# Decoder layers on one core: a first-layer FFN of three products of rounded halves, smaller rings, an expert's weights loaded early

## The reference

```python
# layer 0 (norm first), N_HEAD = 16, DK = 16
h = layernorm(x);  x = x + attn(h, h, causal=True)
h = layernorm(x);  x = x + attn(h, context, causal=False)
h = layernorm(x);  x = x + (relu(h @ ffn_w1 + ffn_b1) @ ffn_w2 + ffn_b2)     # 256 -> 1024 -> 256
# layer 1 (norm last)
x = layernorm(x + attn(x, x, causal=True))
x = layernorm(x + attn(x, context, causal=False))
x = layernorm(x + moe(x))       # router, 2 of 8 experts a row, each gelu(x @ w1 + b1) @ w2 + b2
```

## Time and profile before

| | us |
|---|---|
| median of 3 runs | 1222.42 |
| lowest, highest | 1221.40, 1225.18 |
| the profiled execution | 1223.96 |
| its span (first to last instruction) | 1222.2 |
| TensorE busy in it | 1092.2 (89%) |
| VectorE, ScalarE, GpSimd busy | 823.1, 729.8, 513.1 |

### The profile page before, as it was taken

How to read it: one execution, slowest core, us unless ns; L and a number is a source line. 1 busy time by engine, 2 the same in 40 slices (tenths; PEclk the granted TensorE clock), 3 DMA queues, 4 the chain that set the end, 5 groups by cost and what they waited for, 6 DMA issues and landing times. The chain is left out here.

```text
span 1222.2 us, 26984 instructions
## 1 busy us (share of the span) xinstructions
PE 1092.2 (89%) x8941; PEld 900.1 (74%) x8941; DVE 823.1 (67%) x2495; ACT 729.8 (60%) x1537; POOL 513.1 (42%) x732
## 2 busy tenths in 40 slices
PE   7688889999999999998999988887879999999960
PEld 7366667768887787876777766655669999999960
DVE  2677878775655555546777777764358888888856
ACT  4355565665555455445566666544339888988942
POOL 4355555331222213334667256442242444544544
PEclk9699999999999999999999999987889999999985
DMA  7774848554344434434756645540566878887764
GB/s 176 154 118 75 118 82 108 93 84 59 43 62 65 66 53 54 71 51 56 152 86 93 92 71 92 88 84 28 201 227 204 241 231 231 248 236 232 234 185 146
DMA packets 110313, 152.35 MB, mean 125 GB/s; under 512 B 23040, under 2 KB 94976, under 8 KB 103424
## 3 DMA queue, kind: packets, MB, share of 16 engines
q1 hardware_dynamic: 99984, 138.64, 51.9%
q0 software_dynamic: 8352, 10.80, 4.5%
q10 hardware_dynamic: 1872, 1.60, 1.0%
HBM read 78.39 MB, written 21.62 MB: 82 GB/s over the span
## 5 line engine op out<-in xcount | busy, mean ns | idle before, releaser
L929 ACT ACTIVATE probs<-s 128x384 f32<-128x384 f32 (+1 forms) x512 | 263.7, 542 | 187.5 <-PE s L727 173.4
L1001 DVE TENSOR_REDUCE neg_max<-s 128x2 f32<-128x512 f32 x256 | 169.2, 689 | 94.8 <-PE s L702 89.8
L727 PE MATMUL s<-q_stack,k_stack 98*128 98x256 bf16 (+1 forms) x1024 | 177.1, 263 | 17.4 <-ACT probs L929 16.3
L585 POOL TENSOR_SCALAR_AFFINE_SELECT probs<-probs 128x256 f32<-128x256 f32 x256 | 101.1, 407 | 174.0 <-ACT probs L929 174.0
L998 DVE CUSTOM_DVE_ANT_0 s<-s,mask_qk 128x256 f32<-128x256 f32 x256 | 114.0, 445 | 83.8 <-PE s L699 77.8
L727 PEld LDWEIGHTS s<-q_stack,k_stack 98*128 98x128 bf16 x1024 | 90.8, 99 | 42.9 <-ACT probs L929 27.3
L746 PE MATMUL pv<-probs,v 128*32 128x256 f32 (+1 forms) x2048 | 115.2, 367 | 2.0 <-POOL probs L585 1.8
L1363 PE MATMUL moe<-rows_hi,e_w_hi 128*128 128x256 f32 x368 | 104.1, 283 | 4.1 <-DVE rows_lo L1474 4.1
L702 PE MATMUL s<-k_stack,q_stack 96*128 96x256 bf16 x512 | 98.2, 276 | 10.0 <-DVE neg_max L1001 8.3
L1363 PE MATMUL moe<-e_w_hi,e_hidden_hi 128*128 128x256 f32 x368 | 104.8, 285 | 0.0
L1363 PE MATMUL moe<-rows_hi,e_w_lo 128*128 128x256 f32 x368 | 103.6, 281 | 0.0
(11 more groups left out here) (195 smaller groups left out, 2638.5 us busy)
## 6 DMA issues: line engine op xcount, KB each, us to landing
w<-in_expert_w SPq DMA_DIRECT2D x26, 1024.0 KB, 5.1
k_stack<-k_part SPq DMA_DIRECT2D x192, 128.0 KB, 4.1
e_w<-in_expert_w SPq DMA_DIRECT2D x24, 1024.0 KB, 5.4
q_stack<-q_part SPq DMA_DIRECT2D x180, 128.0 KB, 5.9
rows<-slots_x SPq DMA_DIRECT2D x25, 256.0 KB, 2.7
slots_x<-filler SPq DMA_DIRECT2D x8, 518.0 KB, 4.2
cT<-in_context SPq DMA_DIRECT2D x16, 256.0 KB, 5.3
e_b<-in_expert_b SPq DMA_DIRECT2D x24, 128.0 KB
```

The source lines that it names most:

```text
L585: pool.affine_select(out=blocks, in_=blocks, compare_op=ALU.is_ge, fill=0.0, base=0, pattern=[[0, TILES], [1, P]], channel_multiplier=-1). ...
L727: last = pe.matmul(dst[:, kt * S:kt * S + S - q0], k[:, kt * P:(kt + 1) * P], q[:, q0:S], start=True, stop=True)
L929: act.activation(probs[hd][:, 0:width], s2[hd % 2][:, 0:width], ACT.Exp, scale=SCALE).then_inc(probs_ready, 1)
L1001: dve.tensor_reduce(neg_max[:, :, hd], src[:].rearrange("p (t s) -> p t s", t=TILES), AX_X, ALU.max, negate=True).then_inc(s1_free, 1)
```

## The change

- The FFN's products become three float32r products of halves each, as in the expert part. The weights are halved once, in 8 pieces (`halve`: ScalarE rounds, VectorE subtracts), due beside the last calls of c = 0. The transposed rows (`hT_hi`, `hT_lo`) and the hidden values (`hidden_hi`, `hidden_lo`) are halved for each lane: a rounding on ScalarE and a subtraction on VectorE behind T, and behind each `up`.
- `both_kinds` gives one stretch of memory two names, one float32 and one float32r. The rests are written in place: `w1_lo`, `w2_lo`, `hT_lo` and `hidden_lo` lie over `w1`, `w2`, `hT_ffn` and `hidden`; `w1_hi`, `w2_hi` lie over `w1_next`, `w2_next`. The ReLU of the next lane therefore waits for the last `down` of the lane before.
- To make room: 12 `probs` for 16, 2 contexts for 3, one `h` and one `u` for two, `v` packed to 17 columns a head for 32, the FFN's normed rows in the attention's `o`, and the output biases of c = 2 and 3 loaded over those of c = 0 and 1.
- The weights of expert 1 go into `w1_next`, `w2_next` (the place of the FFN's rounded weights), loaded in four pieces of 512 KB beside calls (3, 2) and (3, 4).
- Due times, lags and paces change, and lane 0 of c = 3 is moved ahead of the last two lanes of c = 2.

```diff
@@ -56,30 +56,32 @@
-CONTEXTS = 3
+CONTEXTS = 2
+PROBS = 12
+VW = DK + 1
...
-LAG = {"scalar": {"T": 0.0, "q": 1.4, "k": 1.7, "v": 1.9, "out_T": 0.1, "up": 1.4, "head": 0.6, "shift": 0.5, "final_T": 0.5, "out": 1.4, "scale": 2.4},
-       "vector": {"max": 0.5, "q": 2.2, "k": 1.9, "shift": 2.8, "wo": 1.6, "down": 0.4, "turn": 0.7, "ln": 0, "apply": 3.6, "router": 0.6, "rank": 1.0, "pick": 0.6,
-                  "place": 0.6},
-       "gpsimd": {"mask": 0.6, "bias": 1.5, "ln": 0, "gain": 3.4, "q": 3.7, "k": 2.9, "scatter": 0},
-       "sync": {"q": 5.2, "k": 5.8, "shift": 0.5, "store": 0.2, "fetch": 0, "context": 0}}
-AT = {"later": 0.0, "pick": 65.9, "place": 68.60000000000001, "shares": (68.5, 71.5, 74.0, 79.3), "fill": 79.0, "ln": -7.3, "T": -1.9, "q": 0.4, "k": -0.8,
-      "v": 6.4, "bias": 10.4, "context": 8.3, "max": 14.8, "shift": 28.3, "head": 32.8, "weigh0": 43.7, "weigh1": 50.0, "turn": 52.5, "out_T": 55.0,
-      "wo": 56.5, "ffn_ln": 59.5, "ffn_T": 62.8, "ffn_bias": 67.4, "up": (68.0, 73.3, 75.1, 76.7), "down": (79.0, 81.5), "final_ln": 59.3, "final_T": 64.7,
-      "store": 63.1, "router": 65.5, "rank": 67.8, "scatter": 85.5, "post_ln": -16.4}
+LAG = {"scalar": {"T": 0.0, "q": 1.4, "k": 1.8, "v": 1.9, "out_T": 0.1, "up": 1.0, "head": 0.6, "shift": 0.8, "final_T": 0.5, "out": 1.4, "scale": 2.4, "halve": 0},
+       "vector": {"max": 0.5, "q": 1.8, "k": 1.9, "shift": 2.8, "wo": 0.4, "down": 0.8, "turn": 0.7, "ln": 0, "apply": 3.1, "router": 0.6, "rank": 1.0, "pick": 0.8,
+                  "place": 0.5, "up": 3.0, "T": 2.0, "halve": 1.0},
+       "gpsimd": {"mask": 0.6, "bias": 0, "ln": 0.5, "gain": 3.1, "q": 3.7, "k": 2.9, "scatter": 0},
+       "sync": {"q": 5.2, "k": 5.8, "shift": 0.5, "store": 0, "fetch": 0.3, "context": 0}}
+AT = {"later": 0.0, "pick": 65.8, "place": 68.6, "shares": (68.5, 71.3, 74.4, 77.0), "fill": 79.0, "ln": -7.5, "T": -1.9, "q": 0.5, "k": -0.8, "v": 6.4,
+      "bias": 13.1, "context": 8.9, "max": 14.8, "shift": 28.1, "head": 32.8, "weigh0": 43.7, "weigh1": 50.0, "turn": 52.5, "out_T": 55.1, "wo": 56.5,
+      "ffn_ln": 59.5, "ffn_T": 62.8, "ffn_bias": 67.4, "up": (65.5, 68.2, 72, 75), "down": (78.5, 81.0), "final_ln": 59.3, "final_T": 64.6, "store": 63.1,
+      "router": 65.5, "rank": 67.8, "scatter": 85.5, "post_ln": -15.0}
...
-PACE = {"max": 0.77, "head": 1.06}
-FETCH = {"w": 5, "ffn": 6.4, "contexts": 2, "qk": 18.0, "vo": 60.0, "expert": 8.2}
-CALL_OF_SLOT = "00000000111111112222222233333333"
+PACE = {"max": 0.71, "head": 1.06}
+FETCH = {"halves": 1.4, "apart": 3.0, "w": 4.5, "ffn": 5.6, "contexts": 0.5, "qk": 21.0, "vo": 60.7, "expert": 8.2}
+CALL_OF_SLOT = "00000000111111112222223223333333"
...
-FFN_LATER = [0.0, 0.0, 0.0, 0.0, 0.0, 0.0, 0.0, 0.0]
+FFN_LATER = [0, 0, 0.0, 0.0, 0, 0, 0, 0.0]
@@ -137,8 +139,10 @@
+    steps += [(at(1, 0) - SLOT * FETCH["halves"] + FETCH["apart"] * i, "halve", 0, i) for i in range(FC)]
...
+    steps += [(at(3, 2 + 2 * i) + 8.0, "fetch", 0, ("second expert", i)) for i in range(KC)]
@@ -238,13 +250,16 @@
-        v = ring(3, "v", [P, TILES, H, 2 * DK])
-        h = ring(2, "h", [P, TILES, D])
+        v = ring(3, "v", [P, TILES * H * VW + 2 * DK - VW])
+        h = sb("h", [P, TILES, D])
...
-        h_of = {FFN: sb("h_ffn", [P, TILES, D])}
-        hT_of = dict.fromkeys((FFN, FINAL), sb("hT_ffn_final", [P, KC, S]))
-        u = ring(2, "u", [P, H // 4, S])
+        (hT_ffn, hT_lo), (hidden, hidden_lo) = both_kinds(ctx, nc, "hT_ffn_final", [P, KC, S]), both_kinds(ctx, nc, "hidden", [P, FC, S])
+        hT_of = dict.fromkeys((FFN, FINAL), hT_ffn)
+        hT_hi, hidden_hi = sb("hT_hi", [P, KC, S], F32R), sb("hidden_hi", [P, FC, S], F32R)
+        (w1, w1_lo), (w2, w2_lo) = w1, w2
+        (w1_next, w1_hi), (w2_next, w2_hi) = w1_next, w2_next
+        u = sb("u", [P, H // 4, S])
@@ -279,11 +294,11 @@
-        probs = ring(H, "probs", [P, TILES * S])
+        probs = ring(PROBS, "probs", [P, TILES * S])
...
+        h_of = {FFN: o}
...
-        hidden = sb("hidden", [P, FC, S])
@@ -385,9 +405,18 @@
+        def piece_of_weights(i):
+            f = slice(2 * (i % 4), 2 * (i % 4) + 2)
+            cols = slice(2 * P * (i % 4), 2 * P * (i % 4 + 1))
+            return (w1[:, :, cols], w1_hi[:, :, cols], w1_lo[:, :, cols]) if i < 4 else (w2[:, f, :], w2_hi[:, f, :], w2_lo[:, f, :])
...
+        def probs_of(n, hd):
+            return probs[(n * H + hd) % PROBS]
@@ -436,6 +465,10 @@
+                elif what[0] == "second expert":
+                    i, half = what[1], FC // 2
+                    sp.dma_start(w1_next[:, i, :], t["expert_w1"][:, KC + i, :]).then_inc(expert_loaded, 16)
+                    sp.dma_start(w2_next[:, i * half:(i + 1) * half, :], t["expert_w2"][:, FC + i * half:FC + (i + 1) * half, :]).then_inc(expert_loaded, 16)
@@ -800,23 +838,29 @@
+            def pair_products(dst, lhs, rhs, first, end):
+                for m, (a, b) in enumerate(((0, 0), (1, 0), (0, 1))):
+                    last = pe.matmul(dst, lhs[a], rhs[b], start=first and m == 0, stop=end and m == 2)
+                return last
             def up(lane, j):
...
-                        pe.wait_ge(loaded_ffn, 16 * 2)
-                    pe.wait_ge(hT_ready, nth("T", lane, FFN))
+                        pe.wait_ge(w_low, FC)
+                    pe.wait_ge(hT_lo_ready, lane + 1)
...
-                        last = pe.matmul(dst[:, m * S:(m + 1) * S], w1[:, k, f * P:(f + 1) * P], hT_of[FFN][:, k, :], start=(k == 0), stop=(k == KC - 1))
+                        last = pair_products(dst[:, m * S:(m + 1) * S], [w[:, k, f * P:(f + 1) * P] for w in (w1_hi, w1_lo)], [r[:, k, :] for r in (hT_hi, hT_lo)], k == 0, k == KC - 1)
...
             def down(lane, i):
...
-                    last = pe.matmul(dst[:, 0:D], hidden[:, f, i * P:(i + 1) * P], w2[:, f, :], start=(f == 0), stop=(f == FC - 1))
+                    last = pair_products(dst[:, 0:D], [part[:, f, i * P:(i + 1) * P] for part in (hidden_hi, hidden_lo)], [w[:, f, :] for w in (w2_hi, w2_lo)], f == 0, f == FC - 1)
@@ -839,6 +883,9 @@
+                if stage == FFN:
+                    act.activation(hT_hi[:], hT_of[FFN][:], ACT.Copy)
+                    act.drain()
@@ -910,23 +957,31 @@
             def up(lane, j):
+                if j == 0 and lane > 0:
+                    act.wait_ge(work_full, filled("down", lane - 1, TILES - 1))
...
-                act.sem_inc(hidden_ready, 1)
+                act.activation(hidden_hi[:, 2 * j:2 * j + 2, :], hidden[:, 2 * j:2 * j + 2, :], ACT.Copy).then_inc(hidden_high, 1)
+            def halve(_, i):
+                if i == 0:
+                    act.wait_ge(loaded_ffn, 16 * 2)
+                w, hi, _ = piece_of_weights(i)
+                act.activation(hi, w, ACT.Copy).then_inc(w_high, 1)
...
-                if hd % HALF == 0:
-                    wait_past(act, weighed, 2 * (n - 1) + hd // HALF + 1)
-                act.activation(probs[hd][:, 0:width], s2[hd % 2][:, 0:width], ACT.Exp, scale=SCALE).then_inc(probs_ready, 1)
+                if hd % HALF == PROBS % HALF:
+                    wait_past(act, weighed, (n * H + hd - PROBS) // HALF + 1)
+                act.activation(probs_of(n, hd)[:, 0:width], s2[hd % 2][:, 0:width], ACT.Exp, scale=SCALE).then_inc(probs_ready, 1)
@@ -960,8 +1015,20 @@
+            o_read, h_read = [0], [0]
+            def take_o(reader):
+                wait_past(dve, work_full, o_read[0])
+                o_read[0] = reader
...
+                if stage == FFN:
+                    take_o(filled("T", lane, FFN))
+                elif stage not in POST:
+                    wait_past(dve, work_full, h_read[0])
+                    h_read[0] = filled("T", lane, stage)
@@ -1032,6 +1100,21 @@
+            def halve(_, i):
+                dve.wait_ge(w_high, i + 1)
+                w, hi, lo = piece_of_weights(i)
+                dve.tensor_tensor(lo, w, hi.bitcast(F32), ALU.subtract).then_inc(w_low, 1)
+            def rest_of_rows(lane, stage):
+                if stage == FFN:
+                    dve.wait_ge(hT_ready, nth("T", lane, FFN))
+                    dve.tensor_tensor(hT_lo[:], hT_of[FFN][:], hT_hi[:].bitcast(F32), ALU.subtract).then_inc(hT_lo_ready, 1)
+            def rest_of_hidden(lane, j):
+                dve.wait_ge(hidden_high, nth("up", lane, j))
+                f = slice(2 * j, 2 * j + 2)
+                dve.tensor_tensor(hidden_lo[:, f, :], hidden[:, f, :], hidden_hi[:, f, :].bitcast(F32), ALU.subtract).then_inc(hidden_ready, 1)
@@ -1238,13 +1321,13 @@
-            fetch_first(1, 1)
+            sp.sem_inc(w1_loaded[1], 16)
...
-            fetch_second(1, 1)
+            sp.sem_inc(w2_loaded[1], 16)
```

68 lines of the change are left out of this document (42 added, 26 removed).

## The result

| | before | after |
|---|---|---|
| median, same chip | 1222.89 (8 runs) | 1218.40 (8 runs) |
| lowest, highest | 1221.11, 1226.12 | 1215.48, 1221.01 |
| profiled execution, span | 1223.96, 1222.2 | 1220.52, 1218.8 |

The ratio is 0.9954, 95% interval 0.9941 to 0.9967: the change gives about 5.6 us (4.5 by the two medians), in the profiled pair 3.4. Forecast were 19.4, with 1193 to 1214 as the range, so the time lies outside it.

What follows compares the result with a forecast made beforehand. The prediction took TensorE to bound the FFN stretches and expert part, with neither TensorE nor VectorE full in c = 0. Terms: -20.3 + 2.5 + 0.5 - 0.6 - 0.5 - 1.0 = -19.4, giving 1203.0 us, range 1193 to 1214.

Steps and rivals of the forecast that it cites:

- The FFN's products: FFN stretches: three float32r instructions replace two per product, saving 2.8 us a lane on TensorE, 20.3 us counted.
- The three quarters for lanes 5 to 7: FFN of lanes 5 to 7, beside causal calls: only three quarters of 8.4 us counted, 6.3 us.
- The changed lags and the order: All calls: changed lags counted at nothing, bounds 8 us either side; moving lane 0 of c = 3 ahead, -1 us.
- Halving the weights: Last calls of c = 0: 8 roundings and 8 subtractions cost 2.5 us, between 0 and 5.5.
- Rings: Calls with fewer buffers, chiefly twelve `probs`: 0.5 us of loss, bounds 0 and 16.
- Rival D: Heads 4 and 12 of each call: twelve `probs` make exponentials wait for `weigh`; slower, 1235; chance 0.06.
- The early load: Start of the expert part: ScalarE's 2.05 us DMA wait goes, gaining 0.6 us, bounds 0 and 2.0.
- Start: Kernel start: filling the narrower `v` ends 1.2 us earlier, gaining 0.5 us (0 to 1.2).
- A: FFN stretches: longer ScalarE and VectorE hops stall TensorE, shrinking them about 1.2 us, not 2.8; 1213; chance 0.12.
- C: New subtractions: VectorE and GpSimd hold each other up, up to 6.8 us more in c = 0; 1210; chance 0.06.
- B: Calls of c = 0, 2 and 3: the new order gives 8 us more than counted; 1195; chance 0.08.
- Signs to look for: Wrong if TensorE idles in FFN stretches, c = 0, 2, 3 calls move over 5 us, or subtractions average over 0.9 us.

Runs made afterwards that it cites:

- e3: The changed kernel with the FFN in plain float32 products again, without any halving: 1232.01 us, ratio 1.0069 to the kernel before.
- e5: The changed kernel with the old order of calls and, for c = 2 and 3, the old due times, lags and pace: 1212.51 us, ratio 0.9877.
- e4: The changed kernel with old due times, lags, paces and fetch times, except the FFN's steps and halving; new order kept: 1240.60 us, ratio 1.0144.
- e9: The changed kernel, new order kept, with the old due times, lags and pace for c = 2 and 3: 1216.35 us, ratio 0.9929.
- e7: The kernel before with two contexts, one h, one u and the FFN's normed rows in the attention's o: 1226.08 us, ratio 0.9992.
- e6: The kernel before with 12 probability buffers for 16 and nothing else: 1225.69 us, ratio 0.9997.
- e1: The changed kernel with the old order of calls, all of c = 2 and then all of c = 3: 1215.86 us, ratio 0.9935.

## Why the prediction was wrong

**The FFN's products: mechanism right, size off.** TensorE bounded these stretches and stayed the bound, the clock was full, the whole effect reached the end, lanes 5 to 7 included (I had taken off a quarter for them; the last three calls of the stage gave 2.2, 1.4 and 2.1 us against e3, the four before 1.9 to 2.2). The step that failed is "that is 0.115 each. A lane has 96 of them too: 11.0 us". The 96 of the earlier trace rows run in a row; the FFN has six blocks a lane between other work, each with a first step of 0.20 to 0.22 us, and 0.118 to 0.119 us for the others. That makes 4 x 1.50 + 2 x 2.95 = 11.9. The six first steps are about 0.5 us of the difference to 11.0, the slower others the rest. The float32 `up` block had no such extra: 1.73 us for 8 is 0.216 with its first step in it. Forecast 2.8 us a lane, measured 1.9; the term is 15.1 (e3) and not 20.3. The three quarters for lanes 5 to 7 were wrong the other way and hid 2.1 us of this. The prediction quoted the Trainium skill ("FP8 and Floating Point Precision", section "TensorE Precision Notes") with four passes for a float32 product, three of which would be 0.75 of it; the blocks show 1.50 to 1.73, 0.87, farther from it than the 0.80 of the prediction. (0.75 would have been 27.6 us of saving by the prediction's own 13.8 a lane, not 27.)

**The changed lags and the order: the larger miss.** "The changed lags I count at nothing, with bounds of 8 us on either side", and "I take -1" for the order. They were +3.6 (the due times and the pace with the lags) and +3.3, and +2.0 together, about 9 us in place of -1. I took the middle of an interval, so the term stood at nothing without a reason. There was one to leave the middle: one table of times serves all four stages, and what is moved for the FFN's steps moves the calls of c = 2 and 3 too, whose times needed no change (e5). Whether the FFN's saving needed the new times in c = 1 no run shows; e4 can't. For the new order I argued that causal calls have more idle time for a lane's ending. They have, but VectorE does its steps in a row, and with a chain of 3.9 us between two maxima TensorE stood for 2.5 (e9). Of the 9.1 us, 4.0 are idle time and 5.1 the same work slower, with 12 us more at the lower clock; the prediction had no term for the clock in these calls.

**Halving the weights.** Forecast 2.5, measured 1.8 (e3). That calls 0 to 9 together came out at +1.9 is in part luck: call 0 is 1.5 longer and call 9 is 2.1 shorter, which has to do with the rings (e7). The call at 162.00 has VectorE at 19.07 of 21.70 beside 16.53 of 20.40 in the earlier trace rows; it was near the bound, as assumed.

**Rings.** Forecast 0.5, measured -0.4 with an interval of -2.2 to 1.5 us for the `probs` (e6) and -1.0 with -2.9 to 1.0 for the others (e7). Rival D with its 1235 had no ground.

**The early load.** Forecast 0.6 by the reasoning that the gelu would next wait for TensorE. The wait of 1.93 us at 904.71 is that one; the gelu came 0.26 to 0.31 us nearer. In the profiled runs the expert part is 1.9 us longer all the same: TensorE's wait ahead of the second tile is 2.53 us, until 924.14 (2.33 in the earlier trace rows), and the clock is low from 925.1 to 928.5, which it wasn't before. e7, the kernel before with other rings and a late load, has such a stretch too (930.6 to 934.1), and e1, with the early load and a wait of 2.50 us, has none, so the load doesn't decide it. What does is open; the 1.9 us are within what such traces differ by, and the 0.6 of the forecast is neither shown nor refuted.

**Start.** The rows that answer to the earlier trace rows:

```profile
9.05 1.57 POOL L590 MEMSET v<- 128x559 f32 x3
12.74 0.74 DVE L1041 TENSOR_SCALAR h<-x,mean_var_main,rstd_main 128x256 f32<-128x256 f32 x2 [4.01 <-POOL rstd_main L569]
```

Filling `v` ends 1.1 us earlier, VectorE's wait 1.05, and the first exponentials come 1.9 us earlier; call 0 takes 23.69 us for 22.16 and gives 1.5 of it back. Net 0.4, forecast 0.5, and that it fits is luck: in e6, which starts as the kernel before does, the first exponentials come at 51.6 us and call 0 takes 22.05, 2.8 us less than before in sum. One pair of traces can't tell this term.

**The rivals.** A (longer hops) didn't happen: in all FFN stretches TensorE waits 3.5 us, and in the three full ones from 299.9 to 397.9 us no product of the FFN waits; its weight loads, which run beside the products, stand 0.6 us in two times for a subtraction of the hidden values. C (VectorE and GpSimd in each other's way) didn't either. VectorE's groups of the halves in 52.4 to 524 us, mean ns in the last but one field:

```profile
L1117 DVE TENSOR_TENSOR hidden_rounded<-hidden,hidden_hi 128x512 fp32r<-128x512 f32 x32 | 22.4, 699 | 2.6 <-ACT hidden_hi L968 0.7
L1107 DVE TENSOR_TENSOR w_rounded<-w,w_next_rounded 128x512 fp32r<-128x512 f32 x8 | 5.6, 705 | 1.3 <-ACT w_next_rounded L974 1.0
L1112 DVE TENSOR_TENSOR hT_ffn_final_rounded<-hT_ffn_final,hT_hi 128x512 fp32r<-128x512 f32 x8 | 5.6, 702 | 0.0
```

About 0.70 us each, against the median of 0.693 in the earlier trace rows. The Trainium skill ("SBUF — State Buffer", section "Who interferes with whom") says that such an instruction, with two inputs in SBUF, contends with one of GpSimd's that reads SBUF; beside a GpSimd that is busy for 8 of 33 us it cost nothing to speak of here. B (the new order gives more) had the sign wrong.

**Signs to look for.** I had named "calls of c = 0, 2 and 3 moved by more than 5 us together" as what would prove me wrong, and it did. The chances gave this case, slower there at an FFN saving that still holds, no place: B and D were its two sides, but D was tied to the rings. The 0.90 for a gain above 3.7 us came true with 5.6, under a third of the forecast.

## What to carry to other kernels

When a change retunes one table of orders for all stages, count each stage that didn't need it as a loss until its calls are compared; here giving c = 2 and 3 their order and times back was worth more (0.9954 to 0.9877) than the change as a whole. Price an instruction from blocks as long as those it will run in, with the first step of a block counted in. Before a chain of small steps is moved on an in-order engine, set its length against what the buffers ahead of TensorE hold at the new place: 3.1 us between two maxima left TensorE idle for 1.3 (e5), 3.2 to 3.9 us for 2.5 (after, e1, e9). And when a table of orders is put back in part, look for pairs of steps that change places by the mixture: e4's 13.5 us of waits are of that kind.
